# Graph network kernel: ranking work spread over the groups of a block, and two thirds of its slot products made in the next block

## The chip, the cores and the metric

The kernel runs on one core of one Trainium2 chip. The metric is the device time of one execution in microseconds (us). The core's engines work side by side, each through its own instructions in order: TensorE (PE in the profile, its weight loads PEld), VectorE (DVE), ScalarE (ACT), GpSimd (POOL) and SyncE (SP), which here only issues DMAs. They wait for one another through semaphores.

## The reference

A graph of 12,500 nodes and 200,000 edges passes through two graph convolutions and one edge network. What matters here is the first convolution's sum over neighbours:

```python
def _sage_conv(x, src, dst, Wl, Wr, b):
    agg = jax.ops.segment_sum(x[src], dst, num_segments=N)
    cnt = jax.ops.segment_sum(jnp.ones((src.shape[0],), x.dtype), dst, num_segments=N)
    mean = agg / jnp.maximum(cnt, 1.0)[:, None]
    return mean @ Wl.T + b + x @ Wr.T

h = jax.nn.relu(_sage_conv(x, src, dst, W1l, W1r, b1))
out = _sage_conv(h, src, dst, W2l, W2r, b2)
```

Edges come sorted by `dst`; `src` is random. Layer norms stand before the convolutions and after them. At the end an edge network computes `relu([h[src], h[dst], edge_attr] @ W1 + b1) @ W2 + b2` for each edge, takes the mean over each source node's edges and adds it to the nodes.

## The kernel before, in words

**Blocks and windows.** The edges are cut into 53 blocks of 3,840 (30 tiles of 128). The nodes are cut into 49 windows of 256. Within a block each edge gets a slot: its window, and its rank among the block's edges whose source lies in that window. So a block's edges stand as a table of 49 windows times 128 slots, and the gather `x[src]` becomes matrix products: a one-hot matrix of slots against the nodes of one window (`hot_t`, made by VectorE at line 1051 from the block's row of source numbers) times the resident node rows (`expand`, line 907), then a second one-hot (`hot_d`, line 1059) times the gathered rows sums them by destination (`reduce`, line 924). ScalarE carries the rows between the two products (`copy_rows`, line 987).

**Groups and steps.** A block of this first convolution (`conv` with `sorting` true) has 7 groups of 7 windows, and each group has 4 steps (windows 2, 2, 2, 1): 28 steps. Step i does `expand(i)` and then `reduce(i - 2)`. Expand and reduce of a whole group are 28 matmuls each. The two one-hots are double buffered. `hot_t` of group g may be overwritten when group g - 2 has been expanded, `hot_d` when group g - 2 has been reduced. In the text G0 to G6 are the moments at which TensorE starts the first step of a group.

**The ranking rides along.** The slots of a block are computed two blocks ahead, by the class `Sorting`, in pieces set between the groups of the block now being summed. For block b + 2, in the order of their dependence: VectorE makes window memberships (`members`, 618); TensorE counts (`count`, 642) and ScalarE keeps the counts; VectorE makes two products `planes` (630); TensorE makes prefix sums in three pieces (`prefix`, 665 and 667, at steps 10, 12 and 14) and ScalarE copies each out (`keep_ranks`, 676); VectorE masks them (`choose`, first instruction, 681) and sums them to a rank (second instruction, 686); VectorE spreads the rank (696) and makes three slot one-hots (`slots`, 703, three instructions); TensorE multiplies each of the three with the planes (`scatter`, 716, ten matmuls each, accumulated in one PSUM bank). In the next block ScalarE takes the result (`take_slots`, 736 to 738), TensorE turns it (`turn`, 726), ScalarE takes the row (`take_row`, 746), SyncE stores it (752) and loads it back broadcast to all partitions (855), and VectorE's one-hots of the block after need it.

**What sets the order.** The order is written out by hand, engine by engine, in `first` and `second` of `conv` (steps 0 to 9 and 10 to 27). A function waits only where its semaphores say so, and everything behind it on the same engine waits with it. Ranking happens only in the first convolution, and only while there is a block b + 2 to rank: in 51 of the 53 blocks (b = 0 to 50), besides two blocks ranked ahead of all. The second convolution runs the same `conv` with `sorting` false.

VectorE's order in a block before the change, with (b+1) for work of the next block: one-hots of group 1, members, `take` (the last block's sums, 1065 to 1069), group 2, both planes, group 3, `add`, group 4, choose and rank sum, group 5, rank spread and all three slot one-hots, group 6, group 0 of b+1.

## Time and profile before

| | |
|---|---|
| median of 3 runs | 4949.99 us (4924.58 to 4953.24) |
| the profiled execution | 4959.75 us, span 4958.0 us |
| busy over the span | PE 82%, DVE 82%, ACT 42%, POOL 49% |
| first convolution with its ranking | from about 193 to about 1555 us |
| mean granted TensorE clock | 0.932 of full speed |

A span is what the hardware profiler saw from first to last instruction; the execution's own time is 1.75 us longer. In a timeline a row stands for one instruction or a run of like ones (x4): start, length, instruction, and in brackets how long the engine had been idle before it and which instruction released it. The starts of successive rows tell more than their lengths, since pipelined instructions overlap.

### The profile page before, as it was taken

Reading aid. Unit: us, or ns where it says so; the run is one execution under the profiler, and the core shown is the slowest. Engines: PE = TensorE matmul, PEld = TensorE weight load, DVE = VectorE, ACT = ScalarE, POOL = GpSimd, SP = SyncE. Lnnn points to the kernel's source line nnn. Section 1 sums busy time; section 2 is a strip of 40 time slices with the busy share of each in tenths; the row PEclk is TensorE's granted clock in tenths of the full one; section 3 lists DMA queues with packets and bytes.
Section 4 is the critical chain, followed back from the end, with each engine's and each line's share of the span. In section 5 each row is a group of like instructions: output and inputs, shape, how many; then the busy total and the mean of one; then the engine's idle time right before and its main releaser. Section 6 shows DMA issues by size and latency. Waiting matters only on the chain. (4 is left out here: it accounts for less than half of the span.)

```text
span 4958.0 us, 186123 instructions
## 1 busy us (share of the span) xinstructions
PE 4089.7 (82%) x71043; PEld 3891.6 (78%) x71043; DVE 4057.1 (82%) x9220; ACT 2065.0 (42%) x4806; POOL 2452.1 (49%) x2144
## 2 busy tenths in 40 slices
PE   0788888888888899999946888888888888888877
PEld 0677777777777799899945888887888888888877
DVE  4588888888886678778775989898989898989985
ACT  1355555555554455556534322222222222322221
POOL 0000000000000688888854777777777777777770
PEclk9999999999997899999977999999989999999986
DMA  2022211222221544454514444444445454444441
GB/s 58 23 67 65 64 63 61 63 65 65 65 65 48 143 107 108 106 107 109 109 32 134 155 154 154 155 154 154 155 155 155 155 155 155 155 154 155 154 120 53
DMA packets 429137, 542.37 MB, mean 109 GB/s; under 512 B 136727, under 2 KB 393935, under 8 KB 428452
## 3 DMA queue, kind: packets, MB, share of 16 engines
q1 hardware_dynamic: 359396, 457.21, 30.7%
q0 software_dynamic: 67840, 77.39, 6.5%
q8 instruction: 431, 7.06, 0.6%
q10 hardware_dynamic: 1426, 0.35, 0.0%
q14 instruction: 44, 0.36, 0.0%
HBM read 462.66 MB, written 72.01 MB: 108 GB/s over the span
## 5 line engine op out<-in xcount | busy, mean ns | idle before, releaser
L1255 POOL DMA_INDIRECT sorted_edges<-edge_rows,edge_index x1590 | 1691.1, 1064 | 572.0 <-issue 476.2
L987 ACT CAST conv_rows<-conv_rows_ps 128x384 bf16<-128x384 f32 (+1 forms) x2597 | 1165.4, 449 | 938.5 <-PE conv_rows_ps L907 925.9
L907 PE MATMUL conv_rows_ps<-parts,conv_hot_t 128*128 128x192 bf16 x9328 | 1202.2, 247 | 189.5 <-DVE conv_hot_t L1051 189.0
L924 PE MATMUL conv_sums<-conv_rows,conv_hot_d 128*128 128x193 bf16 (+1 forms) x9328 | 1205.7, 247 | 48.7 <-DMA conv_got<-parts_table,conv_index 46.6
L1059 DVE TENSOR_TENSOR conv_hot_d<-nodes_b,conv_dst_of 128x1792 bf16<-128x1792 bf16 x742 | 807.9, 1089 | 300.9 <-PE conv_sums L924 299.0
L907 PEld LDWEIGHTS conv_rows_ps<-parts,conv_hot_t 128*128 128x128 bf16 x9328 | 782.1, 98 | 234.6 <-issue 174.8
L924 PEld LDWEIGHTS conv_sums<-conv_rows,conv_hot_d 128*128 128x128 bf16 x9328 | 807.6, 98 | 75.6 <-DMA conv_got<-parts_table,conv_index 73.6
L885 POOL DMA_INDIRECT conv_got<-parts_table,conv_index x530 | 711.4, 1342 | 162.3 <-issue 95.1
L871 POOL MEMSET acc<- 128x6500 f32 x2 | 11.0, 5514 | 1569.8 <-POOLq L440 1569.8
L1319 PE MATMUL edge_sums<-edge_parts,edge_hot 128*128 128x64 bf16 (+1 forms) x15582 | 584.2, 198 | 235.1 <-DVE acc L1481 235.1
L1319 PEld LDWEIGHTS edge_sums<-edge_parts,edge_hot 128*128 128x128 bf16 x15582 | 543.9, 101 | 249.0 <-DVE acc L1481 199.2
L1304 PE MATMUL edge_a_ps<-parts,edge_hot_t 128*128 128x64 bf16 x15582 | 570.1, 199 | 45.3 <-issue 35.7
L1051 DVE TENSOR_SCALAR conv_hot_t<-conv_slot_row,node_of 128x896 bf16<-128x896 bf16 (+2 forms) x1484 | 587.4, 437 | 3.3 <-PE conv_rows_ps L907 0.8
L1304 PEld LDWEIGHTS edge_a_ps<-parts,edge_hot_t 128*128 128x128 bf16 x15582 | 531.1, 102 | 49.7 <-issue 40.0
L1469 DVE TENSOR_SCALAR edge_hot<-nodes_b,edge_src_of 128x256 bf16<-128x256 bf16 x2597 | 541.8, 288 | 0.0
L1364 ACT ACTIVATE edge_parts<-edge_total 128x448 bf16<-128x448 f32 x371 | 216.7, 584 | 662.2 <-DVE edge_total L1456 657.8
L1368 ACT CAST edge_parts<-edge_left 128x448 bf16<-128x448 f32 x371 | 212.2, 572 | 646.2 <-DVE edge_left L1460 640.0
L1285 PE MATMUL edge_rows_ps<-edge_attr_w,edge_attr_t 128*128 128x64 f32 x3180 | 420.2, 286 | 10.9 <-ACT edge_attr_t L1349 6.3
L1481 DVE TENSOR_TENSOR acc<-acc,edge_sums 128x455 f32<-128x455 f32 x742 | 428.0, 617 | 0.7 <-PE edge_sums L1319 0.7
L1285 PEld LDWEIGHTS edge_rows_ps<-edge_attr_w,edge_attr_t 128*128 128x128 f32 x3180 | 413.0, 207 | 13.0 <-ACT edge_attr_t L1349 7.2
L1456 DVE TENSOR_TENSOR edge_total<-edge_a_ps,edge_edges 128x448 f32<-128x448 f32 x371 | 228.5, 616 | 178.3 <-PE edge_a_ps L1304 175.5
L1292 PE MATMUL edge_rows_ps<-edge_b_win,edge_hot_b 128*128 128x64 bf16 x9540 | 345.7, 198 | 0.9 <-issue 0.9
(172 smaller groups left out, 4418.6 us busy)
## 6 DMA issues: line engine op xcount, KB each, us to landing
conv_slot_row<-slot_rows SPq DMA_DIRECT2D x371, 224.0 KB, 3.2
edge_slot_row<-slot_rows SPq DMA_DIRECT2D x371, 224.0 KB
edge_edges<-sorted_edges SPq DMA_DIRECT2D x371, 224.0 KB
edge_dst_row<-dst_rows SPq DMA_DIRECT2D x265, 192.0 KB
edge_attr<-in_edge_attr SPq DMA_DIRECT2D x260, 192.0 KB
conv_slot_row<-slot_rows SPq DMA_DIRECT2D x212, 192.0 KB, 3.2
conv_slot_row<-slot_rows SPq DMA_DIRECT2D x159, 160.0 KB, 3.0
sorted_edges<-edge_rows,edge_index POOLq DMA_INDIRECT x1590
```

Source lines behind the costliest of these rows:

```text
L885: pool.indirect_dma_start(got[g][:, f, :], None, k.parts_table, bass.IndirectOffsetOnAxis(ap=index[h][:, at:at + 1], axis=0)).then_inc(got ...
L907: mm = pe.matmul(rows_ps[i % banks][:, at:at + PARTS * D], hot_t[(h + g) % 2][:, v, u * P:(u + 1) * P], k.parts[:, 2 * (GU * g + u) + v].r ...
L924: mm = pe.matmul(sums[h][:, v * wide_cols:(v + 1) * wide_cols], hot_d[(h + g) % 2][:, u, v * P:(v + 1) * P], row, start=(i == 0 and u == 0 ...
L987: act.copy(rows[i % bufs][:, 0:n, 0:PARTS * D], rows_ps[i % banks][:, 0:n * PARTS * D].rearrange("p (u d) -> p u d", u=n)).then_inc(copied, 1)
L1051: last = dve.tensor_scalar(hot_t[hot][:, v, 0:n_cols], slot_row[g][:, 0:n_cols], k.node_of[:, v:v + 1], None, ALU.is_equal)
L1059: dve.tensor_tensor(hot_d[hot][:].rearrange("p u (n q) -> p u n q", q=QUAD), wide(quads(k.nodes_b[:]), 1, shape), wide(dst_of[h][:, GU * g ...
L1255: pool.indirect_dma_start(k.sorted, bass.IndirectOffsetOnAxis(ap=index[h][0:used, at:at + 1], axis=0), rows[j][0:used, t, :], None).then_i ...
L1285: pe.matmul(rows_ps[to][:, t, :], attr_t[to][:, t // 2, :], k.edge_attr_w[:, t % 2, :], start=(t == 0), stop=False, skip_group_check=True)
L1304: mm = pe.matmul(a_ps[at][:, u, :], hot_t[at][:, v, u * P:(u + 1) * P], k.parts[:, 2 * (GU * j + u) + v, i, :], start=(v == 0 and i == 0), ...
L1319: mm = pe.matmul(to[:, 0:n], hot[at][:, u, v * P:(v + 1) * P], parts[at][:, u, i, 0:n], start=(i == 0), stop=(i == PARTS - 1), skip_group_ ...
L1469: dve.tensor_scalar(hot[at][:, u, :], k.nodes_b[:], src_of[h][:, GU * g + u:GU * g + u + 1], None, ALU.is_equal)
L1481: dve.tensor_tensor(part, part, sums[half][:, 0:GU * D1].rearrange("p (w d) -> p w d", d=D1), ALU.add).then_inc(added, 1)
```

## The change

On VectorE the planes, the rank sum and the slot one-hots become functions of their own and stand behind different groups. Behind group 2 there is one plane; behind group 3 the add and the second plane; behind group 4 only the masking; behind group 5 the rank sum; behind group 6 the spread and the first slot one-hot; and behind group 0 of the next block the other two slot one-hots. On TensorE the first third of the scatter is at step 27, and the other two at steps 1 and 3 of the next block; `turn` moves from step 4 to step 8. On ScalarE `take_slots` moves from step 2 to 6, `take_row` from 5 to 9, `take_dst` from 6 to 9, and `keep_rank` from 24 to 25. No arithmetic and no DMA is added or removed.

```diff
-    def two_planes(self, dve, c, h, n):
+    def plane(self, dve, c, h, n, i):
...
+        if i == 0:
+            if n >= 1:
+
+                dve.wait_ge(self.scattered, c)
+            dve.wait_ge(self.member_made, c + 1)
+        made = dve.tensor_tensor(self.planes[:, :, i, :].rearrange("p t (n q) -> p t n q", q=QUAD), self.member[:].rearrange("p t (n q) -> p t n q", q=QUAD),
+                                 wide(self.number[h][:, 1 + i], 2, shape), ALU.mult)
+        if i:
+            made.then_inc(self.planes_made, 1)
@@
         dve.tensor_tensor(self.ranks[:], self.ranks[:], self.member[:, :, 0:SRC_WINDOWS], ALU.mult).then_inc(self.chosen_made, 1)
+
+    def sum_chosen(self, dve, c, n):
+
         if n >= 1:
@@
-    def slots(self, dve, c, n):
+    def spread_rank(self, dve, c):
...
+    def slots(self, dve, c, n, j):
+
+        if j == 0:
+            if n >= 1:
+
+                dve.wait_ge(self.scattered, c)
+            dve.wait_ge(self.rank_spread, c + 1)
@@ PE, first
-                        if i == 4 and sorts(b, 1):
+                        if i in (1, 3) and sorts(b, 1):
+                            s.scatter(pe, b + 1, n if n == MANY else n + 1, (i + 1) // 2)
+                        if i == 8 and sorts(b, 1):
                             s.turn(pe, b + 1, n if n == MANY else n + 1)
@@ PE, second
-                    if i in (bs - 5, bs - 3, bs - 1):
-                        s.scatter(pe, c, m, (i - bs + 5) // 2)
+                    if i == bs - 1:
+                        s.scatter(pe, c, m, 0)
@@ ACT, first
-                    if i == 2 and sorts(b, 1):
+                    if i == 6 and sorts(b, 1):
                         s.take_slots(act, b + 1, n if n == MANY else n + 1)
-                    if i == 5 and sorts(b, 1):
-                        s.take_row(act, b + 1, n if n == MANY else n + 1)
-                    if i == cut - 4 and (not isinstance(b, int) or b + 1 in range(NB)):
-                        take_dst(b + 1, 1 - h, n if n == MANY else n + 1)
                     if i == cut - 2 and sorts(b, 2):
                         s.keep_earlier(act, b + 2, n if n == MANY else n + 2)
+                    if i == cut - 1 and sorts(b, 1):
+                        s.take_row(act, b + 1, n if n == MANY else n + 1)
+                    if i == cut - 1 and (not isinstance(b, int) or b + 1 in range(NB)):
+                        take_dst(b + 1, 1 - h, n if n == MANY else n + 1)
@@ DVE, first and second
-                    s.two_planes(dve, b + 2, h, m)
+                    s.plane(dve, b + 2, h, m, 0)
...
+                    if g == 3 and sorts(b, 2):
+                        s.plane(dve, b + 2, h, m, 1)
                     if g == 4 and sorts(b, 2):
                         s.choose(dve, b + 2, m)
                     if g == 5 and sorts(b, 2):
-                        s.slots(dve, b + 2, m)
+                        s.sum_chosen(dve, b + 2, m)
+                    if g == 6 and sorts(b, 2):
+                        s.spread_rank(dve, b + 2)
+                        s.slots(dve, b + 2, m, 0)
...
                     make_hot(b + 1, 1 - h, n if n == MANY else n + 1, 0)
+                if sorts(b, 2):
+                    for j in range(1, PIECES):
+                        s.slots(dve, b + 2, m, j)
```

**TensorE at the end of a block.** Before, from step 23 (the last of group 5) to step 27; 716 are the three parts of the scatter, 907 is expand and 924 reduce:

```order
L716 MATMUL conv_slot_ps<-conv_planes,conv_slot_hot 128x98 x10
L907 MATMUL conv_rows_ps<-parts,conv_hot_t 128x192 x4
L924 MATMUL conv_sums<-conv_rows,conv_hot_d 128x193 x4
L907 MATMUL conv_rows_ps<-parts,conv_hot_t 128x192 x4
L924 MATMUL conv_sums<-conv_rows,conv_hot_d 128x193 x2
L716 MATMUL conv_slot_ps<-conv_planes,conv_slot_hot 128x98 x10
L907 MATMUL conv_rows_ps<-parts,conv_hot_t 128x192 x4
L924 MATMUL conv_sums<-conv_rows,conv_hot_d 128x193 x4
L907 MATMUL conv_rows_ps<-parts,conv_hot_t 128x192 x2
L924 MATMUL conv_sums<-conv_rows,conv_hot_d 128x193 x4
L716 MATMUL conv_slot_ps<-conv_planes,conv_slot_hot 128x98 x10
```

After, the end of step 27 and steps 0 to 3 of the next block; the same three parts are line 723, expand is 914 and reduce 931:

```order
L931 MATMUL conv_sums<-conv_rows,conv_hot_d 128x193 x4
L723 MATMUL conv_slot_ps<-conv_planes,conv_slot_hot 128x98 x10
L914 MATMUL conv_rows_ps<-parts,conv_hot_t 128x192 x4
L931 MATMUL conv_sums<-conv_rows,conv_hot_d 128x193 x4
L914 MATMUL conv_rows_ps<-parts,conv_hot_t 128x192 x4
L931 MATMUL conv_sums<-conv_rows,conv_hot_d 128x193 x2
L723 MATMUL conv_slot_ps<-conv_planes,conv_slot_hot 128x98 x10
L914 MATMUL conv_rows_ps<-parts,conv_hot_t 128x192 x4
L931 MATMUL conv_sums<-conv_rows,conv_hot_d 128x193 x4
L914 MATMUL conv_rows_ps<-parts,conv_hot_t 128x192 x2
L931 MATMUL conv_sums<-conv_rows,conv_hot_d 128x193 x4
L723 MATMUL conv_slot_ps<-conv_planes,conv_slot_hot 128x98 x10
```

The scatter's second and third part have moved out of group 6 and behind steps 1 and 3 of the next block. Its first part has moved from ahead of group 6 to behind it.

**VectorE from group 4 to the next block.** Before, from the masking (681) behind group 4's one-hots; 1051 and 1059 are the one-hots of groups 5, 6 and 0 of the next block:

```order
L681 TENSOR_TENSOR conv_ranks<-conv_ranks,conv_member 128x1470
L686 TENSOR_REDUCE conv_rank<-conv_ranks 128x30
L1051 TENSOR_SCALAR conv_hot_t<-conv_slot_row,node_of 128x896 x2
L1059 TENSOR_TENSOR conv_hot_d<-nodes_b,conv_dst_of 128x1792
L696 CAST conv_rank_quads<-conv_rank 128x120
L703 TENSOR_TENSOR conv_slot_hot<-iota_b,conv_rank_quads 128x1280 x3
L1051 TENSOR_SCALAR conv_hot_t<-conv_slot_row,node_of 128x896 x2
L1059 TENSOR_TENSOR conv_hot_d<-nodes_b,conv_dst_of 128x1792
L1051 TENSOR_SCALAR conv_hot_t<-conv_slot_row,node_of 128x896 x2
L1059 TENSOR_TENSOR conv_hot_d<-nodes_b,conv_dst_of 128x1792
```

After, the same stretch; 682 is the masking, 690 the rank sum, 700 the spread, 710 the slot one-hots, 1063 and 1071 the one-hots of groups 5, 6 and 0:

```order
L682 TENSOR_TENSOR conv_ranks<-conv_ranks,conv_member 128x1470
L1063 TENSOR_SCALAR conv_hot_t<-conv_slot_row,node_of 128x896 x2
L1071 TENSOR_TENSOR conv_hot_d<-nodes_b,conv_dst_of 128x1792
L690 TENSOR_REDUCE conv_rank<-conv_ranks 128x30
L1063 TENSOR_SCALAR conv_hot_t<-conv_slot_row,node_of 128x896 x2
L1071 TENSOR_TENSOR conv_hot_d<-nodes_b,conv_dst_of 128x1792
L700 CAST conv_rank_quads<-conv_rank 128x120
L710 TENSOR_TENSOR conv_slot_hot<-iota_b,conv_rank_quads 128x1280
L1063 TENSOR_SCALAR conv_hot_t<-conv_slot_row,node_of 128x896 x2
L1071 TENSOR_TENSOR conv_hot_d<-nodes_b,conv_dst_of 128x1792
L710 TENSOR_TENSOR conv_slot_hot<-iota_b,conv_rank_quads 128x1280 x2
```

The masking and the rank sum now have group 5's one-hots between them, the spread has moved behind group 6, and two slot one-hots have moved behind group 0.

## Rows read from the trace of the kernel before

**Rows 1.** Stretches; busy us (x instructions) per engine, granted clock, DMA share, GB/s.
```profile
220.00:1560.00 1340.00, 1159.25 (x15447) 1054.64 (x15447) 1117.86 (x1800) 762.81 (x2054) 0.00 (x0) 0.99 0.21 64
707.60:732.80 25.20, 21.90 (x297) 19.90 (x295) 21.11 (x34) 14.42 (x40) 0.00 (x0) 1.00 0.20 64
```

**Rows 2.** Groups of instructions, 250 to 1550 us: busy, mean ns, idle before.
```profile
L907 PE MATMUL conv_rows_ps<-parts,conv_hot_t 128*128 128x192 bf16 x5076 | 659.6, 247 | 160.1 <-DVE conv_hot_t L1051 160.1
...
L1059 DVE TENSOR_TENSOR conv_hot_d<-nodes_b,conv_dst_of 128x1792 bf16<-128x1792 bf16 x363 | 394.1, 1086 | 117.4 <-PE conv_sums L924 117.4
```

**Rows 3.** Timeline of TensorE, one block: start, us, engine, line, instruction, idle before.
```profile
700.71 0.50 PE L907 MATMUL conv_rows_ps<-parts,conv_hot_t 128*128 128x192 bf16 x4 [1.71 <-DVE conv_hot_t L1051]
...
704.97 0.50 PE L907 MATMUL conv_rows_ps<-parts,conv_hot_t 128*128 128x192 bf16 x4 [1.32 <-DVE conv_hot_t L1051]
...
708.19 0.49 PE L907 MATMUL conv_rows_ps<-parts,conv_hot_t 128*128 128x192 bf16 x4
...
710.52 0.49 PE L907 MATMUL conv_rows_ps<-parts,conv_hot_t 128*128 128x192 bf16 x4
...
714.09 0.49 PE L907 MATMUL conv_rows_ps<-parts,conv_hot_t 128*128 128x192 bf16 x4
...
717.56 0.49 PE L907 MATMUL conv_rows_ps<-parts,conv_hot_t 128*128 128x192 bf16 x4
...
720.79 0.42 PE L667 MATMUL conv_rank_ps<-conv_earlier,conv_tile_rows 30*128 30x49 bf16 x10
...
721.66 0.49 PE L907 MATMUL conv_rows_ps<-parts,conv_hot_t 128*128 128x192 bf16 x4
...
725.92 0.50 PE L907 MATMUL conv_rows_ps<-parts,conv_hot_t 128*128 128x192 bf16 x4 [1.78 <-DVE conv_hot_t L1051]
```

**Rows 4.** Timeline of VectorE, the same stretch.
```profile
699.77 0.81 DVE L1051 TENSOR_SCALAR conv_hot_t<-conv_slot_row,node_of 128x896 bf16<-128x896 bf16 x2
700.49 1.08 DVE L1059 TENSOR_TENSOR conv_hot_d<-nodes_b,conv_dst_of 128x1792 bf16<-128x1792 bf16 x1
701.50 0.21 DVE L696 CAST conv_rank_quads<-conv_rank 128x120 bf16<-128x120 f32 x1
701.81 2.30 DVE L703 TENSOR_TENSOR conv_slot_hot<-iota_b,conv_rank_quads 128x1280 bf16<-128x1280 bf16 x3
704.03 0.81 DVE L1051 TENSOR_SCALAR conv_hot_t<-conv_slot_row,node_of 128x896 bf16<-128x896 bf16 x2
...
705.76 0.81 DVE L1051 TENSOR_SCALAR conv_hot_t<-conv_slot_row,node_of 128x896 bf16<-128x896 bf16 x2
...
710.56 0.96 DVE L618 TENSOR_TENSOR conv_member<-iota_b,conv_number 128x1560 bf16<-128x1560 bf16 x1
711.44 0.35 DVE L1065 TENSOR_SCALAR conv_moved_to<-iota,shift_to 128x256 f32<-128x256 f32 x1
...
712.24 0.81 DVE L1051 TENSOR_SCALAR conv_hot_t<-conv_slot_row,node_of 128x896 bf16<-128x896 bf16 x2
...
722.34 0.94 DVE L681 TENSOR_TENSOR conv_ranks<-conv_ranks,conv_member 128x1470 bf16<-128x1470 bf16 x1 [1.61 <-ACT conv_ranks L676]
723.38 1.68 DVE L686 TENSOR_REDUCE conv_rank<-conv_ranks 128x30 f32<-128x1470 bf16 x1
724.99 0.81 DVE L1051 TENSOR_SCALAR conv_hot_t<-conv_slot_row,node_of 128x896 bf16<-128x896 bf16 x2
```

**Rows 5.** Timeline of the DMA queue of SyncE, same block.
```profile
712.78 0.32 SPq L752 DMA_DIRECT2D slot_rows<-conv_slot_row  x1
714.27 16.28 SPq L855 DMA_DIRECT2D conv_slot_row<-slot_rows  x7
```

**Rows 6.** The page's DMA issues: KB each, us from issue to landing.
```profile
conv_slot_row<-slot_rows SPq DMA_DIRECT2D x371, 224.0 KB, 3.2
```

**Rows 7.** Two later stretches; columns as in the first group.
```profile
1800.00:2000.00 200.00, 188.94 (x2175) 180.51 (x2176) 158.49 (x290) 118.57 (x278) 163.12 (x122) 0.99 0.49 107
3000.00:4958.00 1958.00, 1625.79 (x38576) 1605.97 (x38572) 1727.72 (x5040) 556.46 (x1142) 1424.63 (x1338) 0.90 0.47 145
```

More of the change, by code:

```diff
@@ L619, in members @@
                           wide(self.number[h][:, 0], 2, shape), ALU.is_equal).then_inc(self.member_made, 1)
-    def two_planes(self, dve, c, h, n):
+    def plane(self, dve, c, h, n, i):
         shape = [P, BT, SRC_COLS // QUAD, QUAD]
-        if n >= 1:
-            dve.wait_ge(self.scattered, c)
-        dve.wait_ge(self.member_made, c + 1)
-        for i in range(2):
-            last = dve.tensor_tensor(self.planes[:, :, i, :].rearrange("p t (n q) -> p t n q", q=QUAD), self.member[:].rearrange("p t (n q) -> p t n q", q=QUAD),
-                                     wide(self.number[h][:, 1 + i], 2, shape), ALU.mult)
-        last.then_inc(self.planes_made, 1)
+        if i == 0:
[6 more added lines that the diff above has]
+            made.then_inc(self.planes_made, 1)
     def count(self, pe, c, n):
@@ L691, in keep_rank @@
         act.copy(self.rank_of[:, bass.ds(c, 1), :].rearrange("p c t -> p (c t)"), self.rank[:]).then_inc(self.rank_kept, 1)
-    def slots(self, dve, c, n):
+    def spread_rank(self, dve, c):
         dve.wait_ge(self.rank_taken, c + 1)
         dve.tensor_copy(self.rank_quads[:], wide(self.rank[:], 2, [P, BT, QUAD])).then_inc(self.rank_spread, 1)
-        if n >= 1:
-            dve.wait_ge(self.scattered, c)
-        dve.wait_ge(self.rank_spread, c + 1)
-        for j in range(PIECES):
-            shape = [P, PT, P // QUAD, QUAD]
-            dve.tensor_tensor(self.hot[:, j * PT:(j + 1) * PT, :].rearrange("p t (n q) -> p t n q", q=QUAD), wide(quads(self.k.iota_b[:]), 1, shape),
-                              wide(self.rank_quads[:, j * PT:(j + 1) * PT, :], 2, shape), ALU.is_equal).then_inc(self.hot_made, 1)
+    def slots(self, dve, c, n, j):
[3 more added lines that the diff above has]
+            dve.wait_ge(self.rank_spread, c + 1)
+        shape = [P, PT, P // QUAD, QUAD]
+        dve.tensor_tensor(self.hot[:, j * PT:(j + 1) * PT, :].rearrange("p t (n q) -> p t n q", q=QUAD), wide(quads(self.k.iota_b[:]), 1, shape),
+                          wide(self.rank_quads[:, j * PT:(j + 1) * PT, :], 2, shape), ALU.is_equal).then_inc(self.hot_made, 1)
     def scatter(self, pe, c, n, j):
@@ L954, in first @@
                 else:
+                    for j in range(1, PIECES):
+                        if sorts(b, 1):
+                            s.scatter(pe, b + 1, n + 1, j)
                     s.count(pe, b + 2, n + 2)
@@ L1026, in second @@
                         s.keep_ranks(act, b + 2, m, (i - cut - 1) // 2)
-                    if i == bs - 4 and sorts(b, 2):
+                    if i == bs - 3 and sorts(b, 2):
                         s.keep_rank(act, b + 2)
@@ L1107, in second @@
                     make_hot(b + 1, 1 - h, n if n == MANY else n + 1, 0)
+                if sorts(b, 2):
+                    for j in range(1, PIECES):
+                        s.slots(dve, b + 2, m, j)
             dve.wait_ge(begun, 2)
```

## The prediction

> **What bounds the kernel now.** The diff touches only the first convolution, so I looked first at the table of stretches, to see what that stage is short of. Over 1340 us of it TensorE shows 1159 us of busy time and VectorE 1118; one period of 25.20 us shows 21.90 and 21.11 at a granted clock of 1.00 [rows 1]. Neither engine is full, and both are near it: the time goes into their waiting for each other by turns. The groups of instructions say for what. TensorE's expands idle 160.1 us for VectorE's `hot_t`, and VectorE's `hot_d` idles 117.4 us for TensorE's reduces [rows 2]. Then I took the timelines of one block, to see where in the block each wait stands.
>
> The block repeats every 25.21 us (700.71 to 725.92, both G5), and its starts on TensorE are [rows 3]: G5 to G6 4.26, G6 to G0 3.22, G0 to G1 2.33, G1 to G2 3.57, G2 to G3 3.47, G3 to G4 4.10, G4 to G5 4.26. G0 to G1 has no ranking work in it and no wait, so **a group of 28 matmuls costs TensorE 2.33 us**. G6 to G0 has two parts of the scatter in it: (3.22 - 2.33) / 2 = 0.44 each. Only two of the seven stretches are longer than TensorE's own work: G4 to G5 by 4.26 - 2.33 = 1.93, and G5 to G6 by 4.26 - 2.33 - 0.44 = 1.49. Together 3.42 us of wait for VectorE per block.
>
> VectorE's rows say why [rows 4]. A pair of one-hots takes 0.72 (`hot_t`, 699.77 to 700.49) and 1.01 (`hot_d`), 1.73 in all. TensorE starts a group 0.94 after the start of its `hot_t` (699.77 to 700.71, 704.03 to 704.97), so 0.22 passes between the end of VectorE's turn and TensorE's start. Ahead of G5 stand the masking and the rank sum, 722.34 to 724.99; ahead of G6 stand the spread (0.31) and three slot one-hots (2.22, so 0.74 each). One-hots are only double buffered, so such a lump cannot be prepared for.
>
> **The change, part by part.** I go round one block, from the masking. Its start does not move against TensorE: it waits for ScalarE's third copy of the prefix sums (idle 1.61), and that follows the prefix at step 14, which ends at 720.79 + 0.42 = 721.21. So it starts 0.68 after G4 (721.66) as before.
>
> - *G4 to G5.* Behind the masking now comes group 5's `hot_t`. What the masking costs when an instruction follows that doesn't need it is not in the trace. Bounds: 1.04, the step to the rank sum that waits for it, and 0.88, members to `moved_to` (710.56 to 711.44), a similar product with an independent follower. I take 0.88. 0.68 + 0.88 + 0.94 = 2.50 against 2.33 of TensorE. Wait left 0.17, where there was 1.93.
> - *G5 to G6.* The rank sum (1.61, 723.38 to 724.99) now stands here, and the 0.44 of scatter that covered part of such a wait has gone from here. 1.73 + 1.61 = 3.34 against 2.33. **Wait left 1.01**, where there was 1.49.
> - *G6 to G0.* 1.73 + 0.31 + 0.74 = 2.78 on VectorE. TensorE has 2.33 and the first third of the scatter, 2.77; its one-hot is ready before step 27 ends (0.94 back, then 1.73 + 0.31 + 0.74 + 0.22 = 2.06 after G6). Equal, wait 0.01.
> - *G0 to G1.* A new wait. The second part of the scatter stands behind step 1, so TensorE comes to it 1.17 after G0 (half a group). Its one-hot is made behind group 0's pair: 1.73 + 0.74 - 0.94 + 0.22 = 1.75 after G0. Wait 0.58, and everything behind it on TensorE waits too, though the expands there could run. The third part comes later than its one-hot. 2.33 + 0.88 + 0.58 = 3.79.
> - *G1 to G2 and on.* VectorE's unbroken run ends its members 1.73 + 1.48 + 1.73 + 0.88 - 0.94 + 0.22 = 5.10 after G0; TensorE reaches the count at 3.79 + 1.17 = 4.96. Wait 0.14. Group 2's `hot_t` starts 0.80 later (`take`, 711.44 to 712.24) and permits G2 at 6.62; TensorE gets there at 7.5 or, with the turn gone to step 8, 7.2. From there VectorE has a lead and the moved second plane lies inside it; `turn` only changes its place between G1 and G3. G1 to G3 7.04 + 0.14, G3 to G4 4.10 as before.
>
> The round is 2.50 + 3.34 + 2.78 + 3.79 + 7.18 + 4.10 = 23.69 us against 25.21, so **1.52 us a block**; waits 3.42 before, 1.91 left. Ranking runs beside 51 blocks: 51 x 1.52 = 78 us. The two blocks ranked ahead of all keep their chain in the same order, and I cost them at nothing. The profiled execution of 4960 would become 4882; the median of the runs lies 10 below that execution, so 4950 - 78 = **4872 us**.
>
> The Trainium skill speaks against one piece of this: "VectorE: DVE Perf Modes", section "The DRAIN you can't avoid", says that a following VectorE instruction waits for the pipeline whether a semaphore stands between them or not. By that rule the masking would still cost 1.04 in its new place and the gain would be 1.36 a block, 69 us, 4881. The rows speak for less than that, the independent pairs starting before the row ahead has ended (710.56 + 0.96 is later than 711.44).
>
> Moved at no cost, with the cover: ScalarE's `take_slots`, `take_row` and `take_dst` come four steps later. The last need for them is the row of source numbers, stored and loaded for group 0 of the next block. Today the store is issued at 712.78, 4.6 after G0, the loads 1.49 later [rows 5], and they land 3.2 after that [rows 6]. Now the store comes at about 7.2 + 0.67 + 0.7 + 0.5 + 0.5 = 9.6 after G0, so the row is there at 14.3, and group 0's `hot_t` wants it at 23.69 - 0.94 = 22.75. Cover 8 us, if it were gone VectorE would be late by what is lacking. The SyncE queue has nothing else to issue there. `keep_rank` and `take_dst` have a whole half block.
>
> **The rivals.**
>
> - *The dearer hand-over.* Work that stood in a row on VectorE now has one-hots between it: five new borders in a block. If each costs the 0.16 between 1.04 and 0.88, 0.8 comes off, the gain is 0.7 a block, 37 us: 4913. Against it: `add` and members stand alone today and cost what their rows say. With the smaller gains around it this covers 4893 to 4945. Chance 0.20.
> - *TensorE becomes the bound.* If VectorE gets ahead, by a masking that starts sooner, the 1.01 and 0.58 shrink. All 3.42 gone would be 174 us, 4776; half of what I leave standing gone gives 1.52 + 0.95 = 2.5 a block, 126 us, 4824. Against it: the third copy of the ranks ties the masking to step 14, and nothing there moves. Chance 0.12.
> - *Nothing happens.* The waits just change places in full: the rank sum as a lump behind group 5 costs what the lumps cost, 4950. Against it: the sum above, in which no stretch gets the whole 1.49 or 1.93 back. Chance 0.06.
> - *Slower, by the clock.* TensorE would be busy 22 of 23.7 us instead of 22 of 25.2. Where it is granted only 0.90 of its clock, as over the last 1958 us [rows 7], its own 21.8 us a block (25.21 - 3.42) become 24.2. TensorE then bounds the block, and with the waits of 1.91 that is up to 26.1, +0.9 a block, +46 us: 4996. It decides from a mean clock below about 0.94 in this stage (21.8 / 0.94 + 1.91 is 25.1). Against it: the second convolution has TensorE busy 188.9 of 200 us at 0.99 [rows 7]. Chance 0.04.
>
> **How the numbers follow.** Forecast (1.3 to 1.9 us a block, 4853 to 4884) with chance 0.58. The likeliest case gives 4872. The range takes in the hand-over's 4913 and the 4824 of the stronger case: 4822 to 4916; outside it lie the strongest gain, the unchanged case and the slow one, and the rest of the first rival. One per cent is 50 us, about what can be told from no change, and the three runs shown spread over 29. Faster by more than that, below 4900: 0.58 + 0.12 + half of the first rival, 0.80. Within it: the other half and the unchanged case, 0.16. Slower: 0.04.
>
> **What would show it.** The period in the timeline: 23.7 us (25.2 if nothing, 22.5 or less for the stronger case). TensorE's idle time for `hot_t`: about 1.0 ahead of G6, nearly none ahead of G5. A new wait of about 0.6 of a scatter matmul for a slot one-hot behind step 1, and a small one of the count for the members. The masking's idle time for ScalarE still near 1.6. No idle of `hot_t` for a DMA. The granted clock still 0.99 or more. The step from the masking to group 5's `hot_t` tells 0.88 from 1.04. TensorE idle in a stretch between G1 and G4 would mean that VectorE did not regain its lead, and my sum is wrong there.

## The result and the profile after

| | before | after |
|---|---|---|
| median of the timed runs | 4937.28 us (4903.24 to 4953.24, 4 runs) | 4865.53 us (4849.09 to 4875.00, 4 runs) |
| the profiled execution | 4959.75 us | 4875.00 us |
| period of one block (mean spacing of the masking's starts, steady blocks) | 25.18 us | 23.54 us |

The ratio is 0.9872, 95% interval 0.9824 to 0.9919: the change makes the kernel faster by 1.3%. The forecast was 4872 us with a block of 23.69. (The median before is now of four runs; the forecast started from 4949.99, the median of three.)

To see where the time went I cut both traces at the first instruction of each stage (the profiled executions, us):

| stage | before | after |
|---|---|---|
| setup and first projection | 199.4 | 169.9 |
| **first convolution** | **1366.4** | **1282.8** |
| norm and projection | 83.8 | 83.7 |
| second convolution | 943.3 | 945.5 |
| norm and projection | 53.6 | 78.3 |
| edge network | 2243.8 | 2245.2 |
| output | 67.7 | 67.8 |

The 83.6 us in the first convolution are the change: 51 blocks times 25.18 - 23.54 = 1.64 us. The 29.5 gained in the setup and the 24.7 lost in the projection ahead of the edge network are not: TensorE's clock stood at another level there, as the last section shows.

The stretches of the stage and of one period, in the columns of [rows 1]:

```profile
220.00:1430.00 1210.00, 1135.82 (x14993) 1018.40 (x14991) 1074.79 (x1747) 732.91 (x1993) 0.00 (x0) 1.00 0.22 69
662.80:686.40 23.60, 22.24 (x295) 19.87 (x294) 20.99 (x35) 14.38 (x40) 0.00 (x0) 1.00 0.24 69
```

A period holds as much TensorE and VectorE work as before (22.24 and 20.99 us busy, 21.90 and 21.11 before) in 1.6 us less, at an unchanged granted clock. So nothing became cheaper; waiting went away. The groups of instructions from 250 to 1450 us, which answer to [rows 2] (there from 250 to 1550 us), say which:

```profile
L914 PE MATMUL conv_rows_ps<-parts,conv_hot_t 128*128 128x192 bf16 x4977 | 647.2, 247 | 46.0 <-DVE conv_hot_t L1063 45.9
...
L1071 DVE TENSOR_TENSOR conv_hot_d<-nodes_b,conv_dst_of 128x1792 bf16<-128x1792 bf16 x355 | 386.5, 1089 | 50.0 <-PE conv_sums L931 43.0
```

TensorE's idle time for `hot_t` fell from 160.1 to 46.0 us. What it waited for in the same stretch, in total, times, and at the longest:

```profile
PE conv_rows_ps L914 <- DVE conv_hot_t L1063: 45.9, 50, 5.8
PE conv_slot_ps L723 <- DVE conv_slot_hot L710: 16.1, 49, 0.4
```

Such a wait stood in two places of a block (102 waits); now it stands in one (50), and a new one, for a slot one-hot, has come beside it in 49 blocks. TensorE's timeline shows both in place; it answers to [rows 3]:

```profile
662.86 0.50 PE L914 MATMUL conv_rows_ps<-parts,conv_hot_t 128*128 128x192 bf16 x4
...
666.18 0.50 PE L914 MATMUL conv_rows_ps<-parts,conv_hot_t 128*128 128x192 bf16 x4 [0.82 <-DVE conv_hot_t L1063]
...
668.97 0.50 PE L914 MATMUL conv_rows_ps<-parts,conv_hot_t 128*128 128x192 bf16 x4
...
670.64 0.62 PE L723 MATMUL conv_slot_ps<-conv_planes,conv_slot_hot 128*128 128x98 bf16 x10 [0.33 <-DVE conv_slot_hot L710]
...
672.70 0.49 PE L914 MATMUL conv_rows_ps<-parts,conv_hot_t 128*128 128x192 bf16 x4
...
673.98 0.94 PE L643 MATMUL conv_count_ps<-conv_member,later_tile 128*30 128x49 bf16 x30
...
679.83 0.49 PE L914 MATMUL conv_rows_ps<-parts,conv_hot_t 128*128 128x192 bf16 x4
...
683.93 0.49 PE L914 MATMUL conv_rows_ps<-parts,conv_hot_t 128*128 128x192 bf16 x4
...
686.41 0.50 PE L914 MATMUL conv_rows_ps<-parts,conv_hot_t 128*128 128x192 bf16 x4
```

The rows of line 914 are G5, G6, G0, G1, G3, G4 and the next G5. The bracket counts only what lies past the modelled end of the matmul before, so it is less than the whole wait: G5 to G6 takes 3.32, which is 0.99 more than the 2.33 of TensorE's own work, where the bracket has 0.82. The scatter's second part could have begun 1.17 after G0, at 670.14, and began at 670.64, 0.50 later.

VectorE's timeline of the same block answers to [rows 4]:

```profile
661.07 0.94 DVE L682 TENSOR_TENSOR conv_ranks<-conv_ranks,conv_member 128x1470 bf16<-128x1470 bf16 x1 [1.61 <-ACT conv_ranks L677]
661.92 0.81 DVE L1063 TENSOR_SCALAR conv_hot_t<-conv_slot_row,node_of 128x896 bf16<-128x896 bf16 x2
...
663.65 1.68 DVE L690 TENSOR_REDUCE conv_rank<-conv_ranks 128x30 f32<-128x1470 bf16 x1
665.25 0.81 DVE L1063 TENSOR_SCALAR conv_hot_t<-conv_slot_row,node_of 128x896 bf16<-128x896 bf16 x2
...
667.29 0.82 DVE L710 TENSOR_TENSOR conv_slot_hot<-iota_b,conv_rank_quads 128x1280 bf16<-128x1280 bf16 x1
668.03 0.81 DVE L1063 TENSOR_SCALAR conv_hot_t<-conv_slot_row,node_of 128x896 bf16<-128x896 bf16 x2
...
669.76 1.56 DVE L710 TENSOR_TENSOR conv_slot_hot<-iota_b,conv_rank_quads 128x1280 bf16<-128x1280 bf16 x2
671.23 0.81 DVE L1063 TENSOR_SCALAR conv_hot_t<-conv_slot_row,node_of 128x896 bf16<-128x896 bf16 x2
```

The lump ahead of G5 is now the masking alone, the one ahead of G6 the rank sum alone. The masking still idles 1.61 for ScalarE's third copy. On SyncE's queue, the store and the loads ([rows 5]):

```profile
678.83 0.32 SPq L759 DMA_DIRECT2D slot_rows<-conv_slot_row  x1
680.31 9.79 SPq L862 DMA_DIRECT2D conv_slot_row<-slot_rows  x7
```

The store is issued 678.83 - 668.97 = 9.86 us after G0, the loads 1.48 later.

### The profile page after: what moved, and what is told of

The parts are those of the page before. It is cut to its first block and busy times, and to the rows that moved or that the text cites. A ratio compares the mean times of both kernels' runs of the same rounds, so it can differ in the third digit from the quotient of the medians.

```text
span 4873.2 us, 186123 instructions
## 1 busy us (share of the span) xinstructions
PE 4098.4 (84%) x71043; PEld 3878.5 (80%) x71043; DVE 4048.4 (83%) x9220; ACT 2065.3 (42%) x4806; POOL 2456.8 (50%) x2144
## 5 line engine op out<-in xcount | busy, mean ns | idle before, releaser
L1324 PEld LDWEIGHTS edge_a_ps<-parts,edge_hot_t 128*128 128x128 bf16 x15582 | 521.3, 101 | 60.1 <-issue 50.4
```

The source lines that it names most:

```text
L1324: mm = pe.matmul(a_ps[at][:, u, :], hot_t[at][:, v, u * P:(u + 1) * P], k.parts[:, 2 * (GU * j + u) + v, i, :], start=(v == 0 and i == 0), ...
```

## The experiments

The theory: within a block TensorE stops only where a lump of ranking work on VectorE stands just ahead of a one-hot, and each piece moved is worth what the sum of durations between two groups says. The general rival: pieces cost more once they stand alone, or the moved work has another effect (clock, DMA), so that the agreement of the sum is chance. Each edit below is against the changed kernel. The block's period is the mean spacing of the masking's starts; where one kernel was traced twice, the two periods agree to 0.01 us, while whole executions of one kernel differ by up to 1.5% (why, at the end). So the mechanism is judged by the period and the worth by the timed runs.

**1. Both planes behind group 2.** Undoes one part.

```diff
-                    if g == 3 and sorts(b, 2):
-                        s.plane(dve, b + 2, h, m, 1)
                     s.plane(dve, b + 2, h, m, 0)
+                    s.plane(dve, b + 2, h, m, 1)
```

> The changed kernel, but both planes stand behind group 2 as before the change. Theory (only VectorE's unbroken run from the masking to group 2 sets the block, behind it VectorE has a lead over TensorE): the block stays at 23.54 us and VectorE only idles less ahead of the masking. Rival (every lump taken off VectorE's order gave its share of the gain, the second plane's 0.88 us among them): the block grows by several tenths, up to 24.4 us.

Measured: period 23.55 us, against 23.54. The plane's place is worth nothing here, as the theory said. (This run came from another chip, where whole times can't be set beside the ones above: one execution of 6638.5 us.)

**2. The rank sum right behind the masking.** Undoes one part.

```diff
                     if g == 4 and sorts(b, 2):
                         s.choose(dve, b + 2, m)
-                    if g == 5 and sorts(b, 2):
                         s.sum_chosen(dve, b + 2, m)
```

> The changed kernel, but the rank sum stands right behind the masking again. Theory (waits along VectorE's unbroken run replace one another): G4 to G5 goes from 2.48 to 4.27 us, but G5 to G6 falls to 2.33, G6 to G0 is 2.77, the wait for the slot one-hot behind step 1 is gone (3.21 instead of 3.72), so the block grows only from 23.54 to about 23.76, 11 us in all. Rival (the split of the masking and the rank sum is where the gain is, since the 1.78 us wait ahead of G5 comes back): the block grows by 0.8 (the 1.78 less the wait of 1.0 that goes ahead of G6) to 1.8 us, 24.3 to 25.3, 40 to 90 us in all.

Measured: period 23.75. The lump has moved back ahead of G5, as VectorE's timeline shows:

```profile
714.13 0.94 DVE L682 TENSOR_TENSOR conv_ranks<-conv_ranks,conv_member 128x1470 bf16<-128x1470 bf16 x1 [1.61 <-ACT conv_ranks L677]
715.17 1.68 DVE L690 TENSOR_REDUCE conv_rank<-conv_ranks 128x30 f32<-128x1470 bf16 x1
716.77 0.81 DVE L1063 TENSOR_SCALAR conv_hot_t<-conv_slot_row,node_of 128x896 bf16<-128x896 bf16 x2
```

and TensorE waits there (1.7 to 1.8 us each) instead of ahead of G6:

```profile
PE conv_rows_ps L914 <- DVE conv_hot_t L1063: 91.1, 50, 5.8
```

The masking's step is 1.04 in front of the sum that waits for it, 0.85 in front of the one-hot. Moving the rank sum apart gives only 0.21 us a block. Timed on two chips: ratio to before 1.0008 (0.9975 to 1.0041) and 1.0012 (0.9983 to 1.0042), with a kernel before at 6616 and 6614 us there. So the gain of the whole kernel is missing on these chips, though the block is 1.43 us shorter than before; experiment 8 takes this up. The repeat below had 74 us less as its theory, and that failed.

> The kernel with the rank sum behind the masking again, whose trace has a block of 23.75 us. Theory: 51 x 1.46 = 74 us less than the kernel before, 11 more than the change. Rival (the gain over the kernel before goes back in later stages): same as the kernel before.

**3. All three slot one-hots behind group 6.** Undoes the move of two of them over the block's border.

```diff
                     if g == 6 and sorts(b, 2):
                         s.spread_rank(dve, b + 2)
-                        s.slots(dve, b + 2, m, 0)
+                        for j in range(PIECES):
+                            s.slots(dve, b + 2, m, j)
...
-                if sorts(b, 2):
-                    for j in range(1, PIECES):
-                        s.slots(dve, b + 2, m, j)
```

> The changed kernel, but all three slot one-hots stand behind group 6, ahead of group 0 of the next block. Theory: G6 to G0 becomes 1.73 + 2.53 = 4.26 us, TensorE having 2.77; G0 to G1 falls from 3.72 to 3.21 as the scatter no longer waits, and the count's 0.11 goes; the block is 24.4 us, 0.85 more, 43 us in all. Rival (the one-hots only have to be off group 5, where they stood before): the block stays within 0.2 us of 23.54.

Measured: period 24.49, +0.95. The second wait for `hot_t` is back, now ahead of G0:

```profile
PE conv_rows_ps L914 <- DVE conv_hot_t L1063: 105.0, 98, 1.3
DVE conv_hot_d L1071 <- PE conv_sums L931: 89.7, 98, 1.1
```

Put back alone, these **two one-hots cost 0.95 us a block** and the rank sum 0.21, of the 1.64 in all. Pieces put back one at a time need not add up, since a wait that goes in one place comes up in another. The moves of the spread and the first one-hot, of the scatter and of ScalarE's work were not undone, so how the remaining 0.48 divides among them is not shown. Ratios to before: 1.0051 (1.0014 to 1.0089) and 1.0072 (1.0031 to 1.0113) on the same two chips: slower than before by 0.5 to 0.7%, with a block 0.69 us shorter.

> The kernel with all slot one-hots behind group 6, whose trace has a block of 24.49 us. Theory: 51 x 0.72 = 37 us less than the kernel before. Rival (given back in later stages): same as the kernel before, or slower.

**4. The row of source numbers much later.** Takes away the cover of 8 us.

```diff
-                    if i == cut - 1 and sorts(b, 1):
-                        s.take_row(act, b + 1, n if n == MANY else n + 1)
...
+                    if i == 23 and sorts(b, 1):
+                        s.take_row(act, b + 1, n if n == MANY else n + 1)
```

> The changed kernel, but ScalarE takes the row of source numbers, and so SyncE stores and loads it, at step 23 instead of step 9. The store then starts about 20.35 us after G0 instead of 9.86. Theory (the row has 8 us of cover in the changed kernel and nothing else hangs on it): the cover is used up, and the block is set by the ring G0, step 23, store (1.48), load (3.3), group 0's one-hot (0.94): 20.35 + 1.48 + 3.3 + 0.94 = 26.1 us, VectorE idle for the DMA ahead of group 0. Rival (the loads of the later groups or the store's own wait bound it earlier or much later): a block above 27, or below 25 us.

Measured: period 27.31, 1.2 more than expected, and by its number inside the rival's range (above 27), though for neither of the rival's reasons. VectorE does wait for the row, and TensorE for VectorE (rows of VectorE, then of TensorE):

```profile
1018.23 0.81 DVE L1063 TENSOR_SCALAR conv_hot_t<-conv_slot_row,node_of 128x896 bf16<-128x896 bf16 x2 [2.37 <-DMA conv_slot_row<-slot_rows]
```

```profile
1016.27 0.60 PE L723 MATMUL conv_slot_ps<-conv_planes,conv_slot_hot 128*128 128x98 bf16 x10
1019.18 0.50 PE L914 MATMUL conv_rows_ps<-parts,conv_hot_t 128*128 128x192 bf16 x4 [2.30 <-DVE conv_hot_t L1063]
...
1020.84 1.00 PE L723 MATMUL conv_slot_ps<-conv_planes,conv_slot_hot 128*128 128x98 bf16 x10
1021.64 0.84 PE L914 MATMUL conv_rows_ps<-parts,conv_hot_t 128*128 128x192 bf16 x4
...
1024.20 0.49 PE L914 MATMUL conv_rows_ps<-parts,conv_hot_t 128*128 128x192 bf16 x4
```

The missing 1.2 us begin at the scatter of 1020.84: after the stop the same ten matmuls take 1.00 instead of 0.60. The stretches before, behind and after it:

```profile
1013.90:1018.20 4.30, 2.94 (x38) 2.79 (x38) 1.86 (x3) 2.07 (x6) 0.00 (x0) 1.00 0.42 135
1019.20:1024.20 5.00, 4.85 (x49) 4.36 (x49) 5.00 (x8) 1.76 (x4) 0.00 (x0) 0.66 0.54 172
1024.20:1029.20 5.00, 5.00 (x78) 4.56 (x76) 4.06 (x9) 2.54 (x9) 0.00 (x0) 1.00 0.00 0
```

The mean granted clock of the 5 us behind TensorE's idle stretch is 0.66: 3.4 us of them lie at the lower of its two levels (1.2 instead of 2.4 GHz), then it is back at full speed. This happens once in each of the 49 blocks of the steady part. G0 to G1 took 1024.20 - 1019.18 = 5.02 instead of 3.73. The ring confirms it: the store is issued 21.50 after G0 instead of the 20.35 expected, and the rest is as expected (1.48 to the loads, 3.30 to the one-hot, 0.95 to TensorE's start):

```profile
1013.45 0.32 SPq L759 DMA_DIRECT2D slot_rows<-conv_slot_row  x1
1014.93 3.82 SPq L862 DMA_DIRECT2D conv_slot_row<-slot_rows  x7
```

(The G0 of that block was at 991.95.) So the row's late landing costs what is lacking, as the prediction said, plus 1.3 us by a lower clock. None of the other kernels shows such a stretch in the steady part of the first convolution: not the changed one, whose longest bracket in a block is 0.82, nor the one before, whose longest is 1.78.

**5. The scatter's second part one step later.** The prediction had a wait of 0.58 in front of it; two theories differ on whether its removal is a gain.

```diff
-                        if i in (1, 3) and sorts(b, 1):
-                            s.scatter(pe, b + 1, n if n == MANY else n + 1, (i + 1) // 2)
+                        if i in (2, 3) and sorts(b, 1):
+                            s.scatter(pe, b + 1, n if n == MANY else n + 1, i - 1)
```

> The changed kernel, but the second part of the scatter stands behind step 2 instead of step 1, by which time its one-hot is there. Theory (VectorE's run behind it sets the time of G2, so the wait only moves): TensorE's 0.50 us wait ahead of this scatter goes, G0 to G1 falls from 3.72 to 3.21, and the count at step 5 waits 0.63 instead of 0.11 for the members: block 23.54 as before. Rival (each wait of TensorE adds to the block): 23.04 us, 26 us less in all.

Measured: period 23.54, nothing gained. TensorE's rows of this kernel show the wait for the slot one-hot gone and one for the members in its place:

```profile
675.06 0.50 PE L914 MATMUL conv_rows_ps<-parts,conv_hot_t 128*128 128x192 bf16 x4
...
676.89 0.60 PE L723 MATMUL conv_slot_ps<-conv_planes,conv_slot_hot 128*128 128x98 bf16 x10
...
680.06 0.93 PE L643 MATMUL conv_count_ps<-conv_member,later_tile 128*30 128x49 bf16 x30 [0.46 <-DVE conv_member L618]
```

The count starts 5.00 after G0, as it did with the earlier scatter (673.98 - 668.97 = 5.01): VectorE's unbroken run from group 6 to the members sets it. Timed 4846.32 us against 4926.53 of the kernel before, ratio 0.9849 (0.9782 to 0.9916).

**6. And the count two steps later too.**

```diff
-                        if i == 5 and sorts(b, 2):
+                        if i == 7 and sorts(b, 2):
                             s.count(pe, b + 2, n if n == MANY else n + 2)
```

> As scatter_later, and the count stands at step 7 instead of step 5. Theory: neither the scatter nor the count waits; what is left of VectorE's run permits G2 6.60 us after G0 (group 2's one-hot starts 5.66 after G0, and 0.94), against 7.04 now: block 23.10 us, 22 us less in all. Rival (the count was not what held it; or the step to the prefix sums becomes tight, since ScalarE keeps the counts at step 8): no gain, 23.5.

Measured: period 23.11, 0.43 less; timed 4821.92 us, ratio 0.9787 (0.9721 to 0.9853). Of TensorE's waits for VectorE in a block only the one ahead of G6 is left:

```profile
PE conv_rows_ps L914 <- DVE conv_hot_t L1063: 45.9, 50, 5.8
PE conv_rank_ps L666 <- ACT conv_ranks L677: 10.2, 49, 0.2
```

Experiments 5 and 6 together show that the 0.5 and the 0.1 were a single wait for VectorE's run, met by whichever of TensorE's instructions came first.

**7. Spread the whole chain.** The reading of all six: no lump of ranking work on VectorE may be longer than TensorE's extra work beside it gives room for, and TensorE's side must come late enough. The slot one-hots stand behind groups 0, 1 and 2, both planes behind 3, the masking behind 4, and the rank sum is cut in halves behind 5 and 6:

```diff
+                if sorts(b, 1):
+                    s.slots(dve, b + 1, n if n == MANY else n + 1, 1)
...
+                if sorts(b, 1):
+                    s.slots(dve, b + 1, n if n == MANY else n + 1, 2)
...
-                    if g == 5 and sorts(b, 2):
-                        s.sum_chosen(dve, b + 2, m)
+                    if g in (5, 6) and sorts(b, 2):
+                        s.sum_chosen(dve, b + 2, m, g - 5)
...
-                        if i in (1, 3) and sorts(b, 1):
-                            s.scatter(pe, b + 1, n if n == MANY else n + 1, (i + 1) // 2)
+                        if i in (3, 7) and sorts(b, 1):
+                            s.scatter(pe, b + 1, n if n == MANY else n + 1, i // 4)
...
+                    if i == cut and n >= 0 and sorts(b, 1):
+                        s.scatter(pe, b + 1, n if n == MANY else n + 1, 2)
```

The count is at step 6, and the take of the slots, the turn, the take of the row, the move of the last block's sums and the take of the destinations follow at steps 12 to 16; on VectorE the last block's sums are taken behind group 2 and added behind group 5.

> A further spreading, by the same theory: the rank sum in two halves, behind groups 5 and 6 (the add with the first half); the rank's spread and the first slot one-hot behind group 0 of the next block, the second behind group 1 with the members, the third behind group 2 with the take; both planes behind group 3. TensorE: scatter at steps 3, 7 and 10 of the next block, count at 6, turn at 13, the move at 15. ScalarE: slots at 12, row at 14, dst at 16. Theory (no piece longer than about 0.6 us plus TensorE's own extra work in that group): waits left of 0.18 ahead of G6, 0.27 ahead of G0, 0.11 ahead of G1; block 22.3 us, 1.24 less than the change, 63 us in all, about 4800. Rival (TensorE and VectorE slow each other or new waits come, above all the row of source numbers, which lands about 18.5 us after G0 with need at 21.4): block 23 us or more.

Measured: period 21.93, first convolution 1202.0 us, 164.4 less than before. Timed 4778.44 us (4721.98 to 4791.97), **ratio 0.9700** (0.9647 to 0.9753). It beats the kernel before, and its interval lies wholly below that of the changed kernel (0.9824 to 0.9919). The same 1000 us from inside the stage, of the kernel before, then of this one:

```profile
300.00:1300.00 1000.00, 870.85 (x11696) 791.30 (x11694) 839.04 (x1353) 573.56 (x1552) 0.00 (x0) 1.00 0.21 65
```

```profile
300.00:1300.00 1000.00, 996.83 (x13388) 907.12 (x13386) 948.83 (x1597) 669.10 (x1780) 0.00 (x0) 1.00 0.23 74
```

TensorE is busy 996.83 of 1000 us, so this stage is now bound by it, and more spreading has nothing left to remove. The expectation was 22.3 a block, with 0.56 of waits left; from 250 to 1350 us the trace has only 2 waits of the expands for `hot_t` where the kernel before has 102 from 250 to 1550 us, so these waits did not come; why not stays open. The period found equals the 21.8 us of TensorE's own work that the prediction subtracted its waits to get (25.21 - 3.42), within 0.14.

A second time, on another chip where the kernel before takes 4929.73 us:

> The same kernel as spread_further, once more. If the chip is one like that of the first runs (kernel before near 4.93 ms): block 21.93 us, first convolution 1202 us, ratio 0.970. If it is one where the kernel before takes 6.6 ms: block 21.93 and first convolution 1202 again (164 less than before there, 1365.6), but the second convolution at 1153 to 1176 us as in every other kernel there against 1078.5 with the kernel before, so about 164 - 90 = 75 us less in all, 1.1%. If the first convolution's gain arrives in full there (160 us, 2.4%), then what the change gave back in the second convolution does not belong to every changed kernel.

4755.08 us (4730.65 to 4786.18), ratio 0.9669 (0.9619 to 0.9719); period 21.92, first convolution 1200.3 us.

**8. Where the gain didn't arrive.** On the two chips of experiments 1 to 4 the kernel before takes 6616 us. I ran both kernels unchanged there.

> The kernel before, once more, beside the change, for its trace on the chip that the others of this group run on. The block 25.2 us, the first convolution 1366 us.

> The changed kernel once more, timed against the kernel before in more rounds. Theory: the first convolution is 51 x 1.67 = 85 us less, all other stages have the same code, and what else differs between two executions is the level at which the small projections run: a median 70 to 95 us below the kernel before, ratio 0.981 to 0.986. Rival (part of the gain is given back in later stages, as two of the variants timed on another chip showed no gain over the kernel before there): ratio above 0.99 and later stages longer in this trace than in that of the kernel before.

Measured for the changed kernel: 6592.15 us (6573.74 to 6634.14, 12 runs) against 6614.41 (26 runs), ratio 0.9990 (0.9961 to 1.0019). Expected were 70 to 95 us less, and that failed; the rival, that part of the gain is given back in later stages, came true. The block gains as everywhere, 25.18 to 23.54, and the first convolution takes 1281.3 instead of 1365.6 us. But the second convolution, whose instructions are the same, takes 1172.4 instead of 1078.5. The same 800 us of it in the kernel before and in the changed one:

```profile
1760.00:2560.00 800.00, 684.71 (x7536) 637.45 (x7537) 547.70 (x1005) 403.12 (x965) 505.30 (x419) 0.96 0.41 93
```

```profile
1760.00:2560.00 800.00, 646.10 (x6878) 588.19 (x6875) 496.36 (x918) 372.40 (x879) 429.97 (x383) 0.95 0.38 85
```

Equal clock, 9% fewer matmuls, and all engines idler at once. GpSimd, which issues the gathers, waits more for the index that ScalarE casts (148.4 us in these 800, 48.3 with the kernel before), and VectorE more for something that the profile can't name ("remote", 175.1 against 63.3). That points to some latency rather than an engine; it is not shown. The other six traces of changed kernels there show 1153 to 1176 us in this stage, the one trace of the kernel before 1078.5. One trace is too few to say that it always gets this, but the timed runs agree: five sets of changed kernels, whose first convolution is 34 to 84 us shorter, come out between 22 us less and 56 us more than the kernel before, so each of them loses 60 to 90 us elsewhere. **Why the second convolution slows there stays open**; no experiment tried it.

## Why the prediction was right

Its steps against the trace of after, in us:

| stretch | forecast | measured |
|---|---|---|
| G4 to G5 | 2.50 | 2.48 |
| G5 to G6 | 3.34 | 3.32 |
| G6 to G0 | 2.78 | 2.79 |
| G0 to G1 | 3.79 | 3.73 |
| G1 to G3 | 7.18 | 7.13 |
| G3 to G4 | 4.10 | 4.10 |
| the block | 23.69 | 23.54 |
| first convolution | 78 less | 83.6 less |

- *The frame* held: the waits sit where VectorE's run since the last group is longer than TensorE's own work. Experiments 1, 2, 3 and 6 changed one such run each, and the period followed the sum to 0.1 us; experiment 5 was to leave it unchanged, and did.
- *The masking with an independent follower*: taken 0.88, measured 0.85 (661.07 to 661.92). The Trainium skill, "VectorE: DVE Perf Modes", section "The DRAIN you can't avoid", says that leaving out a semaphore doesn't avoid the pipeline's flush, and by that the prediction worked out a second sum, with 1.04. The same section also says that a next instruction that is not held back starts earlier, which the prediction left out. The traces side with that sentence: the one-hot starts 0.85 to 0.86 after the masking's start, before the masking's 0.94 are over, and 1.04 stands only in front of the rank sum that waits for the result (experiment 2).
- *The new wait behind step 1* was mis-sized by 0.08: 0.50 instead of 0.58. The hand-over from VectorE to TensorE that I took from `hot_t`, 0.22, is 0.15 for a slot one-hot (made at about 670.49, used at 670.64).
- *The count's wait of 0.14* came out at about 0.1. That it and the wait before it are one and the same limit the prediction didn't say; experiment 5 showed it.
- *The cover of the row*: store forecast 9.6 after G0, measured 9.86. Experiment 4 took the cover away and VectorE was late.
- *The rivals.* "Nothing happens" did not come either: in the changed kernel no lump has its whole wait back. The dearer hand-over did not come (the new borders cost nothing that can be seen, experiment 1). TensorE as the bound came only in experiment 7. The clock rival needed a stage clock under 0.94; it stayed at 1.00 from 220 to 1430 us.
- That 4865.53 lies within 7 us of 4872 is partly luck. The gain between the medians is 71.8 us instead of 78, and the median before came down by 12.7 with its fourth run; the two together make the 6.5. In the profiled executions 83.6 came from the change, and the clock's levels in the small projections took back nearly what they gave (29.5 against 24.7).

## What to carry to other kernels

Where two engines feed one another through double buffers, the mean load of neither tells the time: add up, between each two hand-overs, what either engine must do, and take the larger. A side task should be cut so that no piece exceeds the slack of the stretch it stands in, on the producing engine first; then its consumers on the other engine must be moved late enough, all of them, since a wait that is removed in front of one instruction turns up in front of the next. Judge such a change by the period of its own loop, which here repeats to 0.01 us where the whole kernel scatters by 1.5%.

## What the runs showed of the hardware

**The small projections run at either level of the clock.** The same matmuls took different times in different executions. TensorE's rows at the first projection, before and after:

```profile
120.97 3.17 PE L514 MATMUL conv_in_turn_ps<-ident,conv_in_stage 128*64 128x128 f32 x14 [51.37 <-DVE conv_in_stage L1703]
124.07 3.35 PE L523 MATMUL conv_in_rows_ps<-conv_w,conv_in_h_t 64*128 64x128 f32 x14
```

```profile
119.80 3.17 PE L514 MATMUL conv_in_turn_ps<-ident,conv_in_stage 128*64 128x128 f32 x14 [50.81 <-DVE conv_in_stage L1723]
122.90 1.82 PE L523 MATMUL conv_in_rows_ps<-conv_w,conv_in_h_t 64*128 64x128 f32 x14
```

The first 14 take 3.17 in both; the next 14 take 3.35 or 1.82. The view of this stretch gives a granted clock of 1.00 for both kernels, but for the kernel before that is no reading: its clock record begins only at 218.3 us. For the changed kernel it begins at 122.8, at full speed, just where the matmuls become short. In the other projections the record covers the stage. The one ahead of the edge network, before and after:

```profile
2593.00:2646.00 53.00, 39.03 (x294) 33.75 (x294) 34.30 (x58) 27.49 (x42) 0.00 (x0) 0.89 0.35 95
```

```profile
2482.00:2560.00 78.00, 68.40 (x294) 57.65 (x295) 34.59 (x58) 26.78 (x42) 0.00 (x0) 0.50 0.24 65
```

The same 294 matmuls take 39.03 us at a mean granted clock of 0.89 and 68.40 at 0.50, the lower level (1.2 GHz). TensorE had been idle about 49 us before either. All fourteen traces agree. The second projection takes 84 us at 0.50 and 70.5 at 0.67, the third 78 at 0.50 and 53 at 0.88, the last 68 at 0.50 and 41 to 43 at 0.90. The setup with the first one takes 199 to 200 us in the seven traces whose clock record begins behind it, at 217 to 220 us, and 170 to 172 in the seven where it begins at 122 to 126. (In the kernel before, the 294 matmuls of the first projection take 68.40 us as well, so the lower level there is inferred, not read.) The level does not go with the kernel: experiment 7's had 169.8 us in its first execution traced and 199.9 in the second. What decides it, no run here shows. In all it is worth up to 95 us in 4900, which is enough for the 1.5% by which the runs of one kernel spread.

**The clock after a stop.** An idle stretch of TensorE of 2.3 us was followed by 3.4 us at the lower level (experiment 4). Brackets of 0.82 (the changed kernel) and of up to 1.78 (the kernel before) were not.

**Chips differ.** The same program, the kernel before, takes 4.93 to 4.94 ms where the result and experiments 5 to 7 ran, and 6.62 on the two chips of experiments 1 to 4 and 8. There the first convolution is the same to 1 us (1366.4 and 1365.6), and the edge network takes 3770 us instead of 2244, at a granted clock of 0.74 instead of 0.92 in 3000 to 4800 us; the first row is of the kernel before on the first kind, the second on the other:

```profile
3000.00:4800.00 1800.00, 1510.35 (x36938) 1492.29 (x36934) 1625.41 (x4768) 524.86 (x1094) 1400.24 (x1312) 0.92 0.49 153
```

```profile
3000.00:4800.00 1800.00, 1220.67 (x21602) 1136.55 (x21599) 953.66 (x2787) 310.27 (x639) 778.67 (x774) 0.74 0.33 91
```

TensorE's busy share fell too (1510 to 1221 us of 1800), which a lower clock by itself would not do, so the clock alone is not the reason. What is, no run here settles.
